# Latent attention: a turn laid out in five runs of one array shape, and squared keys and queries summed by one fp32 product each

## The reference

```python
xn = layernorm(x, ln_x_g, ln_x_b)              # the context, 77 tokens a batch
ln = layernorm(latents, ln_l_g, ln_l_b)        # x, 512 tokens a batch
q = (ln @ Wq).reshape(b, m, h, d).transpose(0, 2, 1, 3)
kv = jnp.concatenate([xn @ Wkv, ln @ Wkv], axis=1)
kv = kv.reshape(b, n + m, 2, h, d)
...
qn = rmsnorm(q, qn_g) * scale                  # x / max(|x| / sqrt(64), eps) * gamma
kn = rmsnorm(k, kn_g)
sim = jnp.einsum('bhid,bhjd->bhij', qn, kn)
sim = jnp.where(padded_mask[:, None, None, :], sim, max_neg)
attn = jax.nn.softmax(sim.astype(jnp.float32), axis=-1)
out = jnp.einsum('bhij,bhjd->bhid', attn, v)
return out.reshape(b, m, h * d) @ Wout + bout
```

## Time and profile before

| | us |
|---|---|
| median of 3 runs | 1910.01 |
| lowest and highest | 1908.96, 1915.94 |
| the profiled execution | 1905.26 |
| its span on the core | 1903.4 |
| PE busy, 92% of the span | 1758.1 |
| DVE busy, 77% | 1469.1 |
| ACT busy, 54% | 1032.9 |
| POOL busy, 37% | 701.0 |

### The profile page before, as it was taken

How to read it: one execution, slowest core, us unless ns; L and a number is a source line. 1 busy time by engine, 2 the same in 40 slices (tenths; PEclk the granted TensorE clock), 3 DMA queues, 4 the chain that set the end, 5 groups by cost and what they waited for, 6 DMA issues and landing times. The chain is left out here.

```text
span 1903.4 us, 29213 instructions
## 1 busy us (share of the span) xinstructions
PE 1758.1 (92%) x10747; PEld 1302.9 (68%) x10747; DVE 1469.1 (77%) x2712; ACT 1032.9 (54%) x1570; POOL 701.0 (37%) x571
## 2 busy tenths in 40 slices
PE   5998999689999999999989999899899999989898
PEld 4767888455555655555556777677558889957676
DVE  6887987767767767677668888799799955577798
ACT  3657878457776777767645555455300310055685
POOL 3643221144555555555430444364112302012231
PEclk9998999889999999999989999899999999999899
DMA  2001111100000000000001211000000010000032
GB/s 68 2 15 58 67 67 56 53 1 1 1 1 1 1 1 1 1 1 1 1 20 56 67 67 55 13 1 2 18 17 28 28 56 1 0 13 2 30 111 100
DMA packets 21191, 51.46 MB, mean 27 GB/s; under 512 B 3563, under 2 KB 11383, under 8 KB 18116
## 3 DMA queue, kind: packets, MB, share of 16 engines
q1 hardware_dynamic: 20596, 49.53, 7.6%
q10 hardware_dynamic: 464, 0.20, 0.1%
HBM read 48.48 MB, written 1.25 MB: 26 GB/s over the span
## 5 line engine op out<-in xcount | busy, mean ns | idle before, releaser
L1612 POOL TENSOR_TENSOR sb_L_total<-sb_L_total,sb_L_probT 128x512 f32<-128x512 f32 x128 | 161.4, 1293 | 170.8 <-ACT sb_L_probT L1949 170.8
L441 POOL TENSOR_TENSOR sb_L_prob<-sb_L_prob,sb_L_rsum 128x616 f32<-128x616 f32 (+1 forms) x96 | 105.6, 1121 | 226.3 <-DVE sb_L_rsum L743 226.3
L2017 DVE TENSOR_REDUCE sb_L_tops<-banks 128x2 f32<-128x1024 f32 x128 | 156.4, 1223 | 28.6 <-PE banks L1724 27.0
L1949 ACT ACTIVATE sb_L_probT<-banks 128x1024 f32<-128x1024 f32 x128 | 124.8, 1024 | 80.2 <-PE banks L1759 79.6
L1609 POOL TENSOR_TENSOR sb_L_total<-sb_L_probT 128x512 f32<-128x512 f32 x64 | 93.5, 1484 | 106.0 <-ACT sb_L_probT L1949 106.0
L1772 PE MATMUL banks<-sb_L_probT,sb_L_v 128*64 128x512 f32 x512 | 129.7, 608 | 0.0
L2399 DVE SCALAR_TENSOR_TENSOR sb_L2f_hid<-banks,sb_L2f_weight,sb_L2f_hid 128x512 f32<-128x512 f32 x176 | 122.1, 745 | 3.0 <-PE banks L97 1.6
L2469 DVE SCALAR_TENSOR_TENSOR sb_resid<-banks,sb_L2f_weight,sb_resid 128x128 f32<-128x128 f32 x192 | 67.2, 351 | 62.5 <-PE banks L97 57.9
L1315 DVE TENSOR_TENSOR sb_L0f_hid_low<-sb_L0f_raw,sb_L0f_hid_high 128x1024 fp32r<-128x1024 f32 x64 | 88.6, 1401 | 28.7 <-ACT sb_L0f_hid_high L1271 28.2
L1252 ACT ACTIVATE sb_L1f_gate<-banks 112x512 f32<-112x512 f32 x96 | 57.5, 599 | 91.1 <-PE banks L97 91.1
L529 PE MATMUL banks<-sb_ident,sb_L_prob 128*77 128x128 f32 x640 | 96.5, 284 | 5.8 <-POOL sb_L_prob L441 5.4
(11 more groups left out here) (433 smaller groups left out, 5321.9 us busy)
## 6 DMA issues: line engine op xcount, KB each, us to landing
sb_L0f_wide<-spread_L0f SPq DMA_DIRECT2D x7, 1024.0 KB, 7.7
sb_L1f_wide<-spread_L1f SPq DMA_DIRECT2D x7, 1024.0 KB, 7.3
sb_L3f_wide<-spread_L3f SPq DMA_DIRECT2D x7, 1024.0 KB, 4.8
sb_fetched<-L2f_w SPq DMA_DIRECT2D x12, 256.0 KB, 2.7
sb_fetched<-L1f_gu SPq DMA_DIRECT2D x8, 336.0 KB, 3.1
sb_fetched<-L0f_w SPq DMA_DIRECT2D x8, 259.0 KB, 2.8
sb_fetched<-L0f_w SPq DMA_DIRECT2D x8, 256.0 KB, 3.2
sb_normT<-L2f_w SPq DMA_DIRECT2D x2, 768.0 KB, 4.2
```

The source lines that it names most:

```text
L441: pool.tensor_tensor(grid, grid, bcast(rsum[:, n % PROBS, half], [None, KEYS]), ALU.mult).then_inc(normed, 1)
L1612: pool.tensor_tensor(sums, sums, probT[:, k, h], ALU.add).then_inc(added[h], 1)
L1949: act.activation(probT[:, k], ps[:, slot:slot + 2, :], ACT.Exp).then_inc(exped, 1)
L2017: dve.tensor_reduce(tops[:, :, k, 0], ps[:, banks:banks + 2, :], AX.X, ALU.max).then_inc(bound_read, 1)
```

## The change

Six edits, all in `latent_attention`:

1. The sums of squares, NKL and NQL, are one fp32 product each of the whole squares. The parting (one ACT and one DVE instruction each for keys and for queries) goes.
2. The order on PE. Before, a turn ran rows, columns, full, rows, full, rows, columns: seven runs. Now it runs rows (bound 0, the fifth chunk's scores of the turn before, bound 1, scores 0 and 1, bound 2), columns (products 2 to 4 of the turn before, SUM), full (NKL, Q, V4, KL, the context's work, NQL), rows (bound 3, scores 2 and 3, bound 4), columns (product 0, MT, Y, product 1): five runs. NKC, in one turn of four, still stands among the full ones.
3. Y is written with halved columns: 64 tokens of each 128 in the upper and 64 in the lower half of the output, eight products of 128 x 64 in place of four of 128 x 128.
4. Q is made a turn earlier (turn + 3), with two buffers for the raw and the squared queries.
5. Banks: KL, Q and V4 use banks of the scores that ACT has emptied, SUM shares bank 4 and Y bank 5 with the bounds, KC, NKC and VC bank 6 with the products; the waits follow.
6. ACT, DVE and POOL follow in a new order. On DVE `read_bound(turn + 1, 1)` stands before `finish_sum`, `scale_keys` before bounds 3 and 4 are read, `take_lead` before `scale_queries`, and `add_result` between `scale_queries` and `low_queries` at the turn's end.

The core of the diff:

```diff
                     elif kind == NKL:
-                        pe.wait_ge(k_sq_parted, of + 1)
-                        last = sum_squares(out, k_sq_parts)
+                        pe.wait_ge(k_squared, of + 1)
+                        last = pe.matmul(out, c.pairsum[:], k_sq[:], start=True, stop=True)
...
                         for t in range(TPB):
-                            last = pe.matmul(out[:, t * P:(t + 1) * P], mixedT[:, t * P:(t + 1) * P], wo[:, p, :], start=True, stop=True)
+                            for h in range(2):
+                                last = pe.matmul(out[HEAD[h], t * P:(t + 1) * P], mixedT[:, t * P + h * D:t * P + h * D + D], wo[:, p, :], start=True, stop=True)
...
                     if more:
                         bound(turn + 1, 0)
+                    if turn > 0:
+                        scores(turn - 1, 4)
+                    if more:
+                        bound(turn + 1, 1)
                     scores(turn, 0)
                     scores(turn, 1)
                     if more:
-                        bound(turn + 1, 1)
+                        bound(turn + 1, 2)
...
+                    if turn == 0:
+                        use_side(NQL, 2)
                     product(turn, 0)
                     if more:
                         use_side(MT, turn + 1)
+                    if turn > 0:
+                        use_side(Y, turn - 1)
                     product(turn, 1)
...
                     if much:
-                        part_query_squares(turn + 2)
-                        scale_keys(turn + 2)
-                    if more:
-                        read_bound(turn + 1, 3)
+                        scale_queries(turn + 2)
                     if turn == 1:
                         dve.wait_ge(bias_added, 1)
                     if turn > 0:
```

More of the change, by code:

```diff
@@ L1501, in latent_attention @@
              (V4, 0, 6), (NKL, 1, 2), (NQL, 1, 3), (MT, 0, 4)]
-    SIDES = [(kind, of) for kind, of, _ in EARLY] + [(KL, 2)]
-    for turn in range(TURNS + 1):
+    SIDES = [(kind, of) for kind, of, _ in EARLY] + [(KL, 2), (Q, 2), (V4, 1), (KC, 1), (KL, 3), (Q, 3), (NKL, 2), (NQL, 2), (MT, 1)]
+    for turn in range(1, TURNS + 1):
         extra = {0: KC, 1: NKC, 2: VC}.get(turn % BATCH)
         SIDES += [(kind, of) for kind, of, there in (
[L1506 to L1509, removed]
+            (SUM, turn - 1, True), (NKL, turn + 2, turn + 2 < TURNS), (Q, turn + 3, turn + 3 < TURNS), (V4, turn + 1, turn + 1 < TURNS),
+            (KL, turn + 3, turn + 3 < TURNS), (extra, turn // BATCH + 1, extra is not None and turn // BATCH + 1 < PAIRS and turn < TURNS),
+            (NQL, turn + 2, turn + 2 < TURNS), (MT, turn + 1, turn + 1 < TURNS), (Y, turn - 1, True)) if there]
     BY_DVE = (KL, NKL, Y, MT)
@@ L1713, in bound @@
                             wait_read(pe, MT, turn - 1)
[L1714 to L1719 removed]
+                        if turn >= 3:
+                            wait_read(pe, Y, turn - 3)
+                    if k == 3 and turn > 1:
+                        wait_read(pe, SUM, turn - 2)
                     if banks == 4 and turn + k > 0:
@@ L1849, in _ @@
                     if more:
-                        bound(turn + 1, 3)
-                    if much:
-                        use_side(NQL, turn + 2)
-                    if turn > 0:
-                        use_side(Y, turn - 1)
-                    if more:
                         bound(turn + 1, 4)
-                    scores(turn, 4)
+                    if turn == 0:
+                        use_side(NQL, 2)
                     product(turn, 0)
@@ L1996, in _ @@
-                    exps(turn, 2)
-                    exps(turn, 3)
+                    if turn == 0:
+                        take_v(1)
+                        take_context(1)
+                        square_queries(3)
+                        invert_keys(2)
+                    else:
+                        invert_sum(turn - 1)
+                        if much:
+                            invert_keys(turn + 2)
+                        if turn + 3 < TURNS:
+                            square_queries(turn + 3)
+                        if more:
+                            take_v(turn + 1)
+                        if p + 1 < PAIRS:
+                            if b == 0:
+                                take_context(p + 1)
+                            if b == 1:
+                                invert(NKC, p + 1, kc_inv, kc_inv_ready)
+                            if b == 2:
+                                take_vc(p + 1)
@@ L2144, in _ @@
                         nxt.norm.moments(dve, 0, 2)
-                    if turn % BATCH == 2 and turn // BATCH + 1 < PAIRS:
-                        scale_context(turn // BATCH + 1)
-                    if more:
-                        read_bound(turn + 1, 4)
-                    if much:
-                        scale_queries(turn + 2)
-                    if more:
-                        take_lead(turn + 1)
                     if much:
```

196 lines of the change are left out of this document (97 added, 99 removed).

## The result

The changed kernel takes 1937.95 us in the median of four runs, the kernel before 1912.91 in four beside it. The ratio is 1.0126, with a 95% interval of 1.008 to 1.0172, so it is slower by 1.3%. The prediction was 1928.

A forecast was written before the change was run, and what follows sets the result against it. PE's own sequence was taken to set the pace. A turn gains −0.23 + 0.60 + 0.27 + 0.13 = +0.77: 22.3 over 29 turns, NQL's wait 1.8, edges −6.3, so +17.8 on 1910.0, said as 1928 us; range 1907 to 1943.

The forecast's parts named there:

- my case: The prediction's main case: new waits of about 1.0 us a turn, 1928 us, own range 1917 to 1938, chance 0.58.
- the last rival: "The waits feed one another": late DVE queue or slow Y adds 0.5 us a turn, +32, 1942 us; chance 0.18.
- the rest of the turn: PE's own work in a plain turn: 17.61 + 0.80 − 0.92 − 0.11 = 17.38 us.
- bound 1 behind bound 0: Bound 1 waits on PE until DVE has read bound 0: 1.82 against 1.24 of work, taken as +0.60 us a turn.
- MT behind bound 4: MT waits on PE for DVE's reading of bound 4: 1.77 against 1.50, so +0.27 us a turn, bounds 0.1 and 0.5.
- bound 0 behind `high_queries`: At the turn's end, MT to bound 0 takes 2.40 against PE's 2.27: +0.13 us a turn, bounds 0 and 0.5.
- NQL behind `scale_keys`: NQL's wait on PE: 0.2 us in the nine turns without context work, nothing in others; 1.8 us in all.
- The squares: NKL and NQL: four fp32r products go, two fp32 come, +0.80 us a turn on PE; dropped part instructions worth nothing.
- Two runs fewer: Merged runs on PE: −0.92 us a turn from fewer boundaries and waits, −0.11 from changed start-ups.
- The edges: Turn 0 −2.5, turn 30 −2.8, ahead of turn 0 −1: together −6.3 us, bounds −2 and −9.
- the waits are covered: Rival: PE finds its buffers ready at all four places, turn 17.38, −13 us, 1897 us; chance 0.10.
- only bound 1 waits: Rival: MT and bound 0 stay covered, +0.37 us a turn, +4.4 us, 1914 us; chance 0.14.

The follow-up runs named there:

- e4: The changed kernel with VectorE reading bound 0 over only 256 of the 512 keys in turns 1 to 31; 1927.76 us, ratio 1.008 to the kernel before.
- e3: The changed kernel with `scale_queries` moved ahead of `take_lead` on VectorE; 1930.05 us, ratio 1.0086 to the kernel before.
- e1: The kernel before with only the squares changed to one fp32 product each, its order kept; 1910.9 us, ratio 0.9992.
- e8: The kernel before, its order kept, with fp32 squares in turns 0 to 2 only; 1904.86 us, ratio 0.9964.
- e9: The kernel before, its order kept, with fp32 squares for queries in all turns and for keys in turns 0 to 2; 1900.89 us, ratio 0.9942.
- e5: The changed kernel with Y ahead of MT on TensorE; 1964.87 us, ratio 1.0272 to the kernel before.
- e2: The changed kernel with the squares parted again, so the new order alone; 1935.82 us, ratio 1.0122 to the kernel before.

## Why the prediction was off, step by step

Sign and mechanism were right: slower, by hand-overs that lost their cover, at the places named. The size was 25.0 instead of 17.8, inside the range and between my case and the last rival. The experiments split the plain turn (18.95 measured, 18.58 forecast with NQL's 0.2):

| term | forecast | measured | from |
|---|---|---|---|
| the rest of the turn | 17.38 | 17.57 | 18.95 less the four waits; 0.21 of it is a hand-over to bound 0, see below |
| bound 1 behind bound 0 | 0.60 | 0.54 | 1.82 − 1.28 (e4) |
| MT behind bound 4 | 0.27 | 0.32 | 616.22 − 615.04 − 0.91, and 0.05 in MT itself (0.27 for 0.22) |
| bound 0 behind `high_queries` | 0.13 | 0.32 | 2.63 − 2.31 (e3) |
| NQL behind `scale_keys` | 0.20 | 0.21 | 0.11 late, and 1.05 to bound 3 instead of 0.95 |

**The squares.** +0.80 was forecast and e1 measures +0.77 for the products. But the prediction also put the part instructions at "nothing on the path", since ACT and DVE are idle a quarter of the turn, and that was wrong: in e1 their going takes away 0.49 of wait a turn, and at the start of the stage 4.0 of wait and the low clock behind it. The average idle time of an engine did not say whether the matrix engine waits for it. Taken alone, the product not ahead of or behind a wait is 0.95 less the 0.10 of the change of shape behind it (603.06 to 603.39 before, against 0.23): 0.85, where I took 0.86. The Trainium skill, page FP8 and Floating Point Precision, section TensorE Precision Notes, has four passes for true FP32; at 2.4 GHz that is an estimate of 0.85 for 512 columns, and e1 agrees with its 0.85.

**Two runs fewer, −0.92 and −0.11.** Here 0.19 was missed in the rest of the turn. 0.07 of it is NKL as first in its run: from 607.80 to the third instruction at 609.00 it is 1.20, less 0.23 for the second, so 0.97 where I had 0.86 + 0.04. I had allowed 0.04 for the start-up of a first product where fp32r rows showed 0.11 to 0.12, and fp32 pays as much. 0.04 is bound 0 to bound 1 (1.28 without the wait, 1.24 forecast). The other 0.08 is spread over steps too small to place. Of the 0.92, 0.49 was NQL's wait, which the prediction credited to the merging of runs, and e1 shows that the squares alone remove it. The total is the same, as both parts were made together, but a forecast of either part alone would have been off by it. What the merging of runs itself saves on PE is 17.89 − 17.57 = 0.32 a turn (both hold a hand-over of 0.21, told below), and it brings 1.38 of waits with it. The Trainium skill, page TensorEngine Tiling (Array Packing), section Key Properties, says that a change of tiling mode drains the engine. The trace agrees that it costs, but two runs fewer save only 0.32 here.

**Bound 0 behind `high_queries`: the mis-sized term.** 2.40 was forecast and 2.63 came. On DVE and ACT the chain runs so, DVE first:

```profile
616.70 0.69 DVE L2055 TENSOR_TENSOR sb_L_lead<-banks,sb_L_negblock 128x512 fp32r<-128x512 f32 x1 [0.54 <-PE banks L1650]
617.31 0.69 DVE L2081 SCALAR_TENSOR_TENSOR banks<-banks,sb_L_q_raw 128x512 f32<-128x512 f32 x1
617.91 0.68 DVE L2104 TENSOR_TENSOR sb_resid<-banks,sb_resid 128x512 f32<-128x512 f32 x1
```

```profile
618.03 0.60 ACT L1943 ACTIVATE sb_L_q_high<-banks 128x512 fp32r<-128x512 f32 x1 [1.15 <-DVE banks L2081]
```

From MT it is 0.48 to `take_lead` (0.44 forecast), 0.61 and 0.69 as forecast, 0.03 to ACT, 0.60. That ends at 618.63, and `add_result` at 618.59; bound 0 starts at 618.84, 0.21 and 0.25 later, where I had taken the 0.05 of the earlier trace rows. Bound 1 behind its reading does take 0.05 (601.65 to 601.70).

The longer hand-over stood in rows that I had. In the kernel before, bound 0 waits for `take_lead`, which ends at 611.70 (611.01 + 0.69), and bound 0 starts at 611.96, 0.26 later. It is 0.26 in 28 of 29 turns there. Behind `add_result` it is 0.25 or 0.26 in 27 of 29 turns of the changed kernel and in all 29 of e3. So "nothing waited" before is not what the rows say, and the 1.17 that I took as PE's work behind product 1 is not all work: where no `take_lead` and no `add_result` stand between, it is 0.96, as at the end of turn 30 of the changed kernel (980.35, 981.31):

```profile
980.35 1.03 PE L1788 MATMUL banks<-sb_L_probT,sb_L_v 128*64 128x512 f32 x4
981.31 0.46 PE L1766 MATMUL banks<-sb_L_q_high,sb_L_kc_low 64*77 64x512 f32 x2
```

With 0.26 in place of 0.05 the forecast is 2.61 by the same chain, against 2.63 measured. PE's own work is then 0.21 less than the 17.57 of the table, and bound 0's wait 0.21 more than its 0.32; the kernel before had that 0.21 already. Why it is 0.26 here and 0.05 at bound 1 is open: the instruction at bound 0 waits for several semaphores one after another and stands behind a change of shape, the one at bound 1 does neither, and no run parts the two.

**MT and bound 1.** 1.77 was forecast for bound 4 to MT and 1.79 came; 1.82 to 1.84 for bound 0 to bound 1, and 1.81 to 1.82 came.

**The kinds of turns.** The forecast took +0.77 for every turn with context work. KC and NKC turns got +1.14 and +1.12, VC turns only +0.57. The kernel before already has a wait in its seven VC turns, as this row of it shows:

```profile
664.65 1.08 PE L1772 MATMUL banks<-sb_L_probT,sb_L_v 128*64 128x512 f32 x4
666.06 0.44 PE L1642 MATMUL banks<-sb_ident,sb_L_top_wide 128*64 128x128 f32 x4 [0.32 <-DVE sb_L_top_wide L2021]
```

Product 0 to MT is 1.41, not 0.91, as the scaling of the context stands ahead of the reading of bound 4 on DVE. It is part of MT's 5.0 over 8 times in the earlier trace rows, of which I used only the longest. The new order hides it in a hand-over that every turn now has.

**The edges.** −6.3 was forecast, −5.5 came: −4.3 up to turn 1 (−3.5 forecast) and −1.2 behind turn 29 (−2.8 forecast). The first is right by luck. The wait removed was worth 6.5 us, not 4.0, for the clock behind it (e1), and the order gives 5.0 back by the start of turn 1 (400.94 against 405.96), where I reckoned 1.5. In turn 30 MT's wait fell from 2.8 to the 0.27 of every turn, and the turn is 3.1 shorter: 966.11 to 981.31, with 0.99 for the fifth chunk's scores, which now follow it, against 19.33. But turn 31 and what follows it up to the next block give 2.0 of that back, which the prediction did not weigh; what holds them up was not looked into.

In sum, turns 1 to 29 gave +30.5 where 22.3 + 1.8 was forecast, and the edges −5.5 for −6.3. The prediction held in its sign and in the places of the waits; the sizes of two terms were short, the rest of the turn on PE by 0.19 and bound 0's wait by 0.19 a turn. **The rivals:** "the waits are covered" and "only bound 1 waits" fell, since all four hand-overs wait. "The waits feed one another" named the right direction by the wrong mechanism: bound 0's extra 0.23 did not push bound 1, as e3 shows, and Y with halved columns took 0.87 and not over 1.1.

## What to carry to other kernels

When runs of one shape are merged, count first what the separated order covered: here four hand-overs to VectorE and ACT, 1.38 us a turn, stood against 0.32 us saved by fewer changes of shape. Judge the parts of a change apart, and the stage's first turn apart from the steady ones: the fp32 squares gain 9 us at the start and lose 0.28 a turn, so their best use is at the start (e8), and where they shorten a chain that the matrix engine waits for (e9). A start-to-start time read off the old kernel can hold a hand-over that is no work: 1.17 here, of which 0.96 is work. A wait listed a few times in a table of waits is to be shared out by turn before its longest is taken for all of it.

## What the runs showed of the hardware

- The clock falls behind a stall and stays down for microseconds. In the kernel before, 3.9 us of idle PE are followed by 5.16 us at 0.50, and in six turns of e5 a stall of 1.33 at bound 0 and another at bound 1 are followed by some 3.5 us at 0.51, in the other 23 turns by nothing. The changed kernel has waits of 1.33, 1.31 and 1.22 in turn 0 at a clock of 1.00. By these rows the low clock cost 2.58 us behind the stall of 3.9, and 1.55 behind the two of 1.33 and 0.38: more than half of the stall again, though not always. The Trainium skill, page TensorE: Matmul & The Clock Gate, section Part 1: The HAM clock gate, says that the clock follows how busy TensorE has been lately; the trace agrees as to the fall, with 0.50 and 0.51 behind idle time. Stalls of the same length in the other turns of e5 left it at 1.00.
- The first fp32 product of a run of another shape pays the same start-up as a fp32r one, 0.11 to 0.12, and so does a product whose start was late by a wait: NQL took 1.05 with a wait and 0.95 without.
- The same part instruction on VectorE took 1.48 for the keys and 0.68 for the queries right behind it (e2). It wasn't tried what makes the difference; POOL was adding into `total` at the time.
- From the end of the releasing instruction to the matmul that waits for it is 0.05 us at bound 1 (601.65 to 601.70) and at scores 1 of e4 (598.21 to 598.26), but 0.26 at bound 0 (611.70 to 611.96 before, 596.99 to 597.25 in e3). So the price of a hand-over is to be read at its own place.
